# Row maxima turned by matmuls with an identity in place of DMAs, and a group's keys and queries loaded in three DMAs

## What is computed

```
layer 0:  q = x @ W_q                     4 x 512 x 320
          k, v = text @ W_k, W_v          text: the first 1020 tokens
          p = softmax(q k^T / 4)          per head, 512 x 1020
          text_out = p @ v
          qsem = p @ text                 per head, 512 x 512, then its norm
          4 image tokens: scores q k_ip^T / 4 + 0.5 * cosine(qsem, ip), softmax, times a mask, @ v_ip
          x1 = (text_out + ip_out) @ W_out + b_out + x
layer 1:  the same queries from x1; text is the first 77 tokens, the other 947 are the image part
          x2 = (softmax(text) @ v + softmax(image) @ v_ip) @ Wo^T + bo + x1
```

## Time and profile before

| | |
|---|---|
| time, median of 3 runs | 3732.37 us (3727.62 to 3734.92) |
| the profiled execution | 3733.56 us, its span 3731.7 us |
| TensorE (PE) busy | 3488.6 us, 93% |
| VectorE (DVE) busy | 2116.4 us, 57% |
| ScalarE (ACT) busy | 1689.2 us, 45% |
| GpSimd (POOL) busy | 1059.8 us, 28% |
| mean granted TensorE clock | 0.97 of full speed |
| moved by DMA | 260.59 MB in 636,270 packets |

### The profile page before, as it was taken

One profiled execution on the slowest core, in us unless ns is written; L12 is line 12 of the kernel. 1 busy time (PEld: TensorE's weight loads), 2 busy tenths in 40 slices (PEclk: granted clock), 3 DMA queues, 4 the chain that ended last, 5 costly groups with the idle time before them and its releaser, 6 DMA issues.

```text
span 3731.7 us, 66563 instructions
## 1 busy us (share of the span) xinstructions
PE 3488.6 (93%) x24208; PEld 2894.0 (78%) x24208; DVE 2116.4 (57%) x5503; ACT 1689.2 (45%) x3724; POOL 1059.8 (28%) x889
## 2 busy tenths in 40 slices
PE   5999999998999999999999999999999999999757
PEld 3888878887787877878777787787888888888535
DVE  4444445556555665655656556555655656565657
ACT  0333323444444444535444454444444555555546
POOL 1211011233332322323323222232323222322334
PEclk8999999999999999999999999999999999999878
DMA  4327423236442224226542222423642222222222
GB/s 145 112 61 55 95 67 100 64 61 76 66 112 60 59 61 115 53 52 77 65 115 53 52 62 62 114 50 60 80 55 69 55 47 49 60 52 45 51 62 46
DMA packets 636270, 260.59 MB, mean 70 GB/s; under 512 B 491852, under 2 KB 591004, under 8 KB 635938
## 3 DMA queue, kind: packets, MB, share of 16 engines
q1 hardware_dynamic: 635944, 256.33, 33.3%
HBM read 199.96 MB, written 55.44 MB: 68 GB/s over the span
## 4 chain that ended last, share of the span: by engine, by line
PE 83%; DVE 9%; issue 2%; SPq 2%; DMA 2%; ACT 1%; POOL 1%; POOLq 0%; DVEq 0%; ACTq 0%
PE acc L885 8%; PE acc L892 8%; PE acc L887 8%; PE acc L888 7%; PE acc L893 7%; PE acc L886 6%; PE score L855 4%; PE score L936 3%; PE spare L936 3%; PE av L923 3%; PE score L857 3%; PE av L927 3%; PE score L972 3%; PE spare L1008 2%; PE spare L972 2%
## 5 line engine op out<-in xcount | busy, mean ns | idle before, releaser
L1077 ACT ACTIVATE prob<-score 128x512 f32<-128x512 f32 x1219 | 729.6, 599 | 1747.1 <-PE score L857 1746.3
L1377 POOL TENSOR_TENSOR prob_lo<-prob,prob_hi 128x512 fp32r<-128x512 f32 x593 | 776.1, 1310 | 1577.7 <-ACT prob_hi L1080 1577.2
L885 PE MATMUL acc<-tok_v,prob_hi 128*128 128x300 f32 x2240 | 936.1, 418 | 6.0 <-DMA tok_v<-v_scr 5.6
L892 PE MATMUL acc<-tok_v,prob_lo 128*128 128x278 f32 (+1 forms) x2560 | 750.1, 293 | 6.2 <-DVE prob_lo L1140 6.2
L887 PE MATMUL acc<-tok_lo,prob_hi 128*128 128x256 f32 (+1 forms) x2560 | 744.4, 291 | 0.4 <-POOL tok_lo L1406 0.4
L1080 ACT ACTIVATE prob_hi<-score 128x512 fp32r<-128x512 f32 x1219 | 726.4, 596 | 0.0
L888 PE MATMUL acc<-tok_lo,prob_hi 128*128 128x256 f32 (+1 forms) x2560 | 721.9, 282 | 0.0
L893 PE MATMUL acc<-tok_v,prob_lo 128*128 128x256 f32 (+1 forms) x2560 | 720.2, 281 | 0.0
L886 PE MATMUL acc<-tok_v,prob_hi 128*128 128x256 f32 x2240 | 631.4, 282 | 0.0
L1140 DVE TENSOR_TENSOR prob_lo<-prob,prob_hi 128x512 fp32r<-128x512 f32 x687 | 502.4, 731 | 85.7 <-ACT prob_hi L1080 85.6
L885 PEld LDWEIGHTS acc<-tok_v,prob_hi 128*128 128x128 f32 x2240 | 433.0, 193 | 85.7 <-issue 58.7
(11 more groups left out here) (265 smaller groups left out, 5011.0 us busy)
## 6 DMA issues: line engine op xcount, KB each, us to landing
k_ring<-k_scr SPq DMA_DIRECT2D x960, 64.0 KB
tok_v<-v_scr SPq DMA_DIRECT2D x160, 176.0 KB, 3.3
v_ring<-v_scr SPq DMA_DIRECT2D x160, 148.5 KB, 3.3
ctx_t<-in_ctxT SPq DMA_DIRECT2D x8, 2048.0 KB, 9.3
q_ring<-q_scr SPq DMA_DIRECT2D x960, 16.0 KB
v_scr<-v_stage SPq DMA_DIRECT2D x32, 440.0 KB, 2.5
k_scr<-part_bf SPq DMA_DIRECT2D x32, 384.0 KB, 2.6
v_scr<-v_stage SPq DMA_DIRECT2D x36, 330.0 KB, 9.8
```

Of the source, the lines that this page charges most:

```text
L885: e.matmul(out_a[:, 0:SEG + VCOLS], p_hi, tok_v[0:kk, c, seg, v_lo:v_lo + SEG + VCOLS], start=first, stop=False)
L892: e.matmul(out_a[:, v_one:v_one + SEG + VH], p_lo, tok_v[0:kk, c, seg, v_lo + v_one:v_lo + v_one + SEG + VH], start=False, stop=False)
L1077: e.activation(prob[:, es, :], bank_s[:, :], ACT.Exp, scale=SCALE)
L1377: e.tensor_tensor(prob_lo[:, ps, :], prob[:, es, :], prob_hi.bitcast(F32)[:, ps, :], ALU.subtract).then_inc(s_low[1], 1)
```

## The change

The rows of maxima: `neg_max` is now split into its three parts while the queries still lie on the 128 partitions. The parts go to columns 96 to 98 (or 101) of `row_parts`, 102 columns of which the rest are zero, for each of the 4 rows. Step max_rows becomes four matmuls with a bf16 identity, whose result has each part on its own partition, 96 to 101, and 512 columns wide; one copy by VectorE brings it into `q_ring`. `max_t`, `max_bf` and the DMAs go.

Loads and stores: `q_scr` and `k_scr` hold all six products for each dimension, in the order (dimension, product), so a group's keys are one load of 96 rows, its queries another, and its constant rows a third. A store of parts becomes three DMAs: with `Q_RUNS` part 0 is written three times, part 1 twice and part 2 once; with `K_RUNS` parts 0 to 2, then 0 and 1, then 0.

The spans of the maxima change as well. At the start a bf16 identity and the zeros of `row_parts` are made.

```diff
-MAX_SPAN = {"lead": (8, 6), "woven": (11, 11), "tail": (8, 16)}
+MAX_SPAN = {"lead": (8, 4), "woven": (12, 7), "tail": (8, 9)}
...
+Q_RUNS = ((0, 3, 0), (3, 5, 1), (5, 6, 2))
+K_RUNS = ((0, 3), (3, 5), (5, 6))
...
-        q_scr = scratch("q_scr", (2 * B, 3, D, SQ), BF16)
-        k_scr = scratch("k_scr", (2 * BATCHES, 3, D, T), BF16)
+        q_scr = scratch("q_scr", (2 * B, D, 6, SQ), BF16)
+        k_scr = scratch("k_scr", (2 * BATCHES, D, 6, T), BF16)
...
@@ TensorE, first chunk of a group @@
                         e.wait_ge(s_qk[slot], qk_ready[g])
-                        e.wait_ge(s_rows[slot], rows_ready[g])
+                        e.wait_ge(s_free, job["max_rows", g] + 1)
...
@@ TensorE, step max_rows @@
-                    n_rows = MR * (layer + 1)
+                    n_rows = 96 + 3 * (layer + 1)
                     e.wait_ge(s_neg, nth["neg", g] + 1)
                     bg = bank_free(*s)
-                    e.transpose(bg[0:n_rows, 0:P], neg_max[:, layer, 0:layer + 1, :].rearrange("p a b -> p (a b)"),
-                                ident[:]).then_inc(s_bg, 1)
+                    for r in range(MR):
+                        mm = e.matmul(bg[0:n_rows, r * P:(r + 1) * P], row_parts[:, layer, r, 0:n_rows], ident_bf[:], start=True, stop=True)
+                    mm.then_inc(s_bg, 1)
...
@@ VectorE, constants @@
+                    e.tensor_copy(ident_bf[:], ident[:]).then_inc(s_mem, 1)
+                    e.memset(row_parts[:], 0.0).then_inc(s_mem, 1)
...
@@ VectorE, step split @@
-                        e.wait_ge(s_part[i % 2], 16 * (i // 2))
+                        e.wait_ge(s_part[i % 2], 48 * (i // 2))
...
@@ VectorE, step neg, behind the reduce @@
+                    value, rest = neg_max[:, layer, 0:layer + 1, :], max_r[:, layer, 0:layer + 1, :]
+                    part = row_parts[:, layer, :, 96:96 + 3 * (layer + 1)].rearrange("p r (k i) -> p i k r", i=3)
+                    e.wait_ge(s_mx, i0 + 1)
+                    e.tensor_copy(part[:, 0], value).then_inc(s_mx, 1)
+                    e.wait_ge(s_mx, i0 + 2)
+                    e.tensor_tensor(rest, value, part[:, 0], ALU.subtract).then_inc(s_mx, 1)
+                    e.wait_ge(s_mx, i0 + 3)
+                    e.tensor_copy(part[:, 1], rest).then_inc(s_mx, 1)
+                    e.wait_ge(s_mx, i0 + 4)
+                    e.tensor_tensor(part[:, 2], rest, part[:, 1], ALU.subtract).then_inc(s_neg, 1)
...
@@ VectorE, step max_rows @@
-                    e.tensor_copy(max_t[0:n, :], bank[bank_of[s]][0:n, 0:P]).then_inc(s_free, 1)
-                    e.tensor_copy(bf[:, 0, :], max_t[0:n, :]).then_inc(s_mx, 1)
-                    e.tensor_tensor(max_r[0:n, :], max_t[0:n, :], bf[:, 0, :], ALU.subtract).then_inc(s_mx, 1)
-                    e.tensor_copy(bf[:, 1, :], max_r[0:n, :]).then_inc(s_mx, 1)
-                    e.tensor_tensor(bf[:, 2, :], max_r[0:n, :], bf[:, 1, :], ALU.subtract).then_inc(s_mx, 1)
+                    e.tensor_copy(q_ring[rows, slot, :, :].rearrange("p j t -> p (j t)"), bank[bank_of[s]][rows, :]).then_inc(s_free, 1)
...
@@ SP, step lower @@
-                    e.dma_start(dst, part_bf[0:w, i % 2, :, 0:n]).then_inc(s_part[i % 2], 16)
+                        for lo, hi, j in Q_RUNS:
+                            e.dma_start(q_scr[u, rows, lo:hi, :],
+                                        part_bf[0:w, i % 2, j:j + 1, 0:SQ].broadcast_to([w, hi - lo, SQ])).then_inc(s_part[i % 2], 16)
+                        for lo, hi in K_RUNS:
+                            e.dma_start(k_scr[u // PARTS, rows, lo:hi, 512 * key[3]:512 * key[3] + 512],
+                                        part_bf[0:w, i % 2, 0:hi - lo, :]).then_inc(s_part[i % 2], 16)
...
@@ SP, step load_qk @@
-                    for j in range(GROUP):
-                        e.dma_start(k_ring[96:102, slot, j, :], row_scr[:, layer, :]).then_inc(s_qk[slot], 16)
-                    for i in range(6):
-                        rows = slice(DH * i, DH * i + DH)
-                        e.dma_start(k_ring[rows, slot, :, :],
-                                    k_scr[u // PARTS, K_PARTS[i], h0 * DH:(h0 + GROUP) * DH, :].rearrange("(h d) t -> d h t", d=DH)).then_inc(s_qk[slot], 16)
-                        e.dma_start(q_ring[rows, slot, :, :],
-                                    q_scr[u, Q_PARTS[i], h0 * DH:(h0 + GROUP) * DH, :].rearrange("(h d) t -> d h t", d=DH)).then_inc(s_qk[slot], 16)
+                    at = slice(h0 * DH, (h0 + GROUP) * DH)
+                    e.dma_start(k_ring[96:102, slot, :, :],
+                                row_scr[:, layer, :].rearrange("p (o t) -> p o t", o=1).broadcast_to([6, GROUP, T])).then_inc(s_qk[slot], 16)
+                    e.dma_start(k_ring[0:96, slot, :, :],
+                                k_scr[u // PARTS, at, :, :].rearrange("(h d) i t -> (d i) h t", d=DH)).then_inc(s_qk[slot], 16)
+                    e.dma_start(q_ring[0:96, slot, :, :],
+                                q_scr[u, at, :, :].rearrange("(h d) i t -> (d i) h t", d=DH)).then_inc(s_qk[slot], 16)
...
@@ SP, step max_rows @@
-                    for k in range(layer + 1):
-                        for i in range(3):
-                            row = 96 + 3 * k + i
-                            e.dma_start(q_ring[row:row + 1, slot, :, :].rearrange("p j (s c) -> p (j s) c", c=P),
-                                        max_bf[MR * k:MR * k + MR, layer, i, :]).then_inc(s_rows[slot], 16)
```

More of the change, by code:

```diff
@@ L24 @@
 WINDOW = 4
[L25 to L26 removed]
+PRODUCTS = 6
+Q_RUNS = ((0, 3, 0), (3, 5, 1), (5, 6, 2))
+K_RUNS = ((0, 3), (3, 5), (5, 6))
 VH = 22
@@ L608, in cross_attention_pair @@
     group_nth = [sum(1 for x in range(g) if x % RING == g % RING) + 1 for g in range(len(seq))]
-    row_loads_of = [3 if UNITS[u][0] == 0 else 6 for u, _ in seq]
-    rows_ready = [16 * sum(row_loads_of[x] for x in range(g % RING, g + 1, RING)) for g in range(len(seq))]
-    qk_ready = [16 * 14 * x for x in group_nth]
+    qk_ready = [16 * 3 * x for x in group_nth]
     score_name = ["score0" if n < tail + 3 or (n - tail) % 2 else "acc1" for n in range(len(chunks))]
@@ L675, in cross_attention_pair @@
         MR = GROUP * ST
-        max_t = sb("max_t", [2 * MR, P])
-        max_r = sb("max_r", [2 * MR, P])
-        max_bf = sb("max_bf", [2 * MR, 2, 3, P], BF16)
+        max_r = sb("max_r", [P, 2, 2, MR])
+        row_parts = sb("row_parts", [P, 2, MR, 102], BF16)
+        ident_bf = sb("ident_bf", [P, P], BF16)
         ip_scores = sb("ip_scores", [P, 2, ST, HEADS, IP])
@@ L1247, in _ @@
                     if layer == 0:
-                        e.tensor_reduce(neg_max[:, layer, 0, :], mp[:, :, 0:2], AX_X, ALU.max, negate=True).then_inc(s_neg, 1)
+                        e.tensor_reduce(neg_max[:, layer, 0, :], mp[:, :, 0:2], AX_X, ALU.max, negate=True).then_inc(s_mx, 1)
                     else:
                         e.tensor_scalar(neg_max[:, layer, 0, :], mp[:, :, 0], -1.0, None, ALU.mult)
-                        e.tensor_reduce(neg_max[:, layer, 1, :], mp[:, :, 1:3], AX_X, ALU.max, negate=True).then_inc(s_neg, 1)
+                        e.tensor_reduce(neg_max[:, layer, 1, :], mp[:, :, 1:3], AX_X, ALU.max, negate=True).then_inc(s_mx, 1)
@@ L1252, in _ @@
+                    e.wait_ge(s_mx, i0 + 3)
+                    e.tensor_copy(part[:, 1], rest).then_inc(s_mx, 1)
+                    e.wait_ge(s_mx, i0 + 4)
+                    e.tensor_tensor(part[:, 2], rest, part[:, 1], ALU.subtract).then_inc(s_neg, 1)
                 elif kind == "max_rows":
                     g = s[1]
-                    layer = UNITS[seq[g][0]][0]
-                    n, i = MR * (layer + 1), nth[s]
-                    bf = max_bf[0:n, layer, :, :]
+                    layer, slot = UNITS[seq[g][0]][0], ring_of(g)
@@ L1257, in _ @@
+                    rows = slice(96, 96 + 3 * (layer + 1))
                     e.wait_ge(s_bg, job[s] + 1)
-                    if g in same_before:
-                        e.wait_ge(s_rows[ring_of(same_before[g])], rows_ready[same_before[g]])
-                    e.tensor_copy(max_t[0:n, :], bank[bank_of[s]][0:n, 0:P]).then_inc(s_free, 1)
-                    e.wait_ge(s_free, job[s] + 1)
-                    e.tensor_copy(bf[:, 0, :], max_t[0:n, :]).then_inc(s_mx, 1)
-                    e.wait_ge(s_mx, 4 * i + 1)
@@ L1505, in _ @@
                                         v_scr[u // PARTS, :, :, c0:c0 + V1].rearrange("b p v -> p b v")).then_inc(s_v[turn % V_SLOTS], 16)
-                elif kind == "max_rows":
-                    g = s[1]
-                    layer, slot = UNITS[seq[g][0]][0], ring_of(g)
-                    e.wait_ge(s_mx, 4 * nth[s] + 4)
-                    for k in range(layer + 1):
-                        for i in range(3):
-                            row = 96 + 3 * k + i
-                            e.dma_start(q_ring[row:row + 1, slot, :, :].rearrange("p j (s c) -> p (j s) c", c=P),
```

(5 more changed lines are left out.)

19 lines of the change are left out of this document (8 added, 11 removed).

## The result

The changed kernel takes 3768.39 us (median of 4 runs, 3765.54 to 3771.69) against 3733.39 us of the kernel before (4 runs): the ratio is 1.0097 [1.0079, 1.0114]. It is 35 us slower, where 26 us less were forecast, and above the range. The profiled execution has a span of 3763.9 us.

The account below looks back on a forecast made before the run. TensorE was taken as the bound, busy 3255 of 3377 us in the long stage. Loads -19, start -6, matmuls +25, tail -22 and spans -4 gave -26 us against 3733.6, so 3706 us; range 3680 to 3731.

Parts of the forecast that it names:

- The spans: New due times of the maxima: last unit's lead stops growing, sharing VectorE's lateness over more slots; -4 us (-8 to +8).
- The cover: Slot between "neg" and max_rows hides maxima reaching TensorE 0.75 us later; where missing, mostly in the tail, waits grow 0.75 us.
- The loads: Three DMA issues a group instead of 14, 1.3 us instead of 6.4: long stage -19 us, start -6 us.
- the change doesn't save issue time: Rival on SP's queue: one issue of 96 partitions costs as much as the six it replaces; 3742 us, chance 0.04.
- The tail: Last two units of layer 1: waits for loads and row DMAs shrink; -22 us (-34 to -12).
- The four matmuls: max_rows on TensorE: 0.28 us for four, +0.17 a group over the transpose; +25 us over 145 groups.
- the load sets the pace: Rival on max_rows: weight loads of 99 and 102 columns limit the matmuls, +33 us for +25; 3714 us, chance 0.15.
- nothing overlaps: Rival on max_rows: load and matmul run one after the other, +0.47 us a group, +68 us; 3749 us, chance 0.10.
- the copy: VectorE's copy of 512 columns from PSUM into q_ring: 690 ns where the old copy took 277, +0.4 us.
- the four steps: VectorE's small split steps, now ahead of TensorE on 128 partitions: 0.2 us each where they had about 0.3.

Follow-up runs that it names:

- run 1: The changed kernel with the old spans (8, 6), (11, 11), (8, 16): 3711.26 us, 0.9919 of the kernel before.
- run 10: The changed kernel with old lead and tail spans and the woven span at (12, 11), only its length new: 3708.63 us, 0.9906 of the kernel before.
- run 9: The changed kernel with old lead and tail spans and the woven span at (11, 7), only its margin new: 3812.07 us, 1.0189 of the kernel before.
- run 3: The changed kernel, new spans kept, with max_rows two slots behind "neg" in place of one: 3723.76 us, 0.9957 of the kernel before.
- run 7: The changed kernel with the old spans and max_rows two slots behind "neg": 3682.99 us, 0.9832 of the kernel before.
- run 4: The kernel before with only the three loads a group and three stores a split; rows and spans as before: 3695.85 us, 0.9881.

## Why the prediction was wrong

**The step that failed** is "The spans": "-4 (-8 to +8, since in the long stage other pairs of jobs will meet in the two banks, and the waits for VectorE there come and go)". They cost +61.3 us: +52.7 in the woven stage, +9.5 in the tail, -1.2 in the lead and +0.3 in the start (after against run 1). I had reasoned about the tail, for which the new numbers are gentler, and gave the woven stage, three quarters of the kernel, half a bracket. With it falls the sentence ahead of it: "The cover is the slot between 'neg' and 'max_rows'; where it is missing, the wait grows by 0.75 us. That is mostly in the tail." The mechanism was named and its place was wrong. The cover was also taken for a constant, when the spans in the same diff set it: the order of the steps is fixed by `plan()`, so the work of TensorE between each "neg" and its max_rows can be added up from the list before anything runs. At about 0.72 us for a step "mix", 0.47 for "av1" and so on, a layer 1 group of the woven stage has a median of 3.1 us there with the old spans, 1.8 us with the new ones (14 groups under 0.6 us), 1.4 us with the margin of 7 and length 11, and 3.1 again with length 12 and margin 11. These are estimates, and they go with the times: runs 1 and 10 are fast, after is slow, run 9 slowest. The traces bear them out. From the start of "neg" on VectorE to the end of TensorE's work ahead of max_rows the 129 groups of the woven stage have a mean of 3.75 us in run 1, 3.61 in run 10, 2.06 in after and 1.54 in run 9; from the same start to the end of L1265 VectorE needs a mean of 1.5 to 1.7 us in all four. Under 1.5 us are 14 groups in run 1, 20 in run 10, 50 in after and 74 in run 9. The groups of L945 by form, in the woven stage of after (102 columns is layer 1, 99 is layer 0):

```profile
L945 PE MATMUL score<-ident_bf,row_parts 128*99 128x128 bf16 x168 | 17.3, 227 | 20.5 <-DVE row_parts L1265 14.1 <-DVE max_parts L1238 5.9
L945 PE MATMUL score<-ident_bf,row_parts 128*102 128x128 bf16 x148 | 15.3, 227 | 20.7 <-DVE row_parts L1265 20.7
L945 PE MATMUL spare<-ident_bf,row_parts 128*102 128x128 bf16 x112 | 11.6, 226 | 24.1 <-DVE row_parts L1265 24.1
L945 PE MATMUL spare<-ident_bf,row_parts 128*99 128x128 bf16 x88 | 9.8, 238 | 19.9 <-DVE row_parts L1265 13.6 <-DVE max_parts L1238 5.9
```

and of run 1:

```profile
L945 PE MATMUL spare<-ident_bf,row_parts 128*102 128x128 bf16 x172 | 17.3, 224 | 4.7 <-DVE row_parts L1265 4.6
L945 PE MATMUL spare<-ident_bf,row_parts 128*99 128x128 bf16 x148 | 15.4, 226 | 7.3 <-DVE row_parts L1265 7.2
L945 PE MATMUL score<-ident_bf,row_parts 128*99 128x128 bf16 x104 | 10.8, 226 | 4.7 <-DVE row_parts L1265 4.5
L945 PE MATMUL score<-ident_bf,row_parts 128*102 128x128 bf16 x92 | 9.1, 222 | 3.3 <-DVE row_parts L1265 3.3
```

Layer 1 waits 44.8 us for L1265 where run 1 has 7.9, as its shorter slot says. Layer 0 waits 27.7 us where run 1 has 11.7, though by the same count its median slot grows, from 0.95 to 1.8 us. The trace shows why the count misleads there: VectorE starts "neg" a mean of 2.05 us before TensorE comes to max_rows, where run 1 has 2.70, and it isn't held up longer from there on (1.55 us to the end of L1265, where run 1 has 1.72). It comes later to "neg"; what in its order makes it late no run shows.

The count tells what stands in the slot, too. With the old spans 30 of the 65 groups of layer 1 have four steps "mix", one "max" and one "av1" between "neg" and max_rows. With the new ones 14 have a single "av1" there, and 14 more two "mix" and the "av1".

What the new spans cost beyond these waits is open in part. With two slots they still lose 42 us (the spans of run 3 and run 7), and the waits for L1265 are then nearly equal (34.4 and 32.3 us). Of that, 33.2 us are in the woven stage, 11.6 as TensorE's busy time and 21.6 as idle. Over the span L853 waits 31.1 us in place of 7.1, and 15.4 against 1.7 of that is the wait for the copy L1271 (run 3). L934 waits about as long for VectorE to take the maxima, only for other ones of them: 33.2 us (24.0 for L1238 and 9.2 for L1240), where run 7 has 31.3 (6.4 and 24.9). The busy time and the rest of the idle time no run takes apart. It also means that the 60 us of waits for L1265 and the 61 us of loss agree only with one slot between "neg" and max_rows.

**The loads: right.** Three issues take from 34.98 to 36.13 us, 1.15 us where I said 1.3, in SP's queue of after at the start:

```profile
34.98 0.30 SPq L1485 DMA_DIRECT2D k_ring<-row_scr  x1
35.31 0.34 SPq L1487 DMA_DIRECT2D k_ring<-k_scr  x1
35.69 0.44 SPq L1489 DMA_DIRECT2D q_ring<-q_scr  x1
```

In run 4 the start is 7.8 us shorter (forecast 6), the woven stage 16.3 (forecast 19). The rival that the change doesn't save issue time is out: 96 partitions cost what 16 did. The stores write 23.6 MB more (79.04 in place of 55.44 MB; 199.96 MB are read in both), and no run shows a cost of that. One reading was off by little: the earlier trace rows counts the 1.7 us to the landing of a store from its start, and I counted them from its end. The store of x1 that I had landing at 1889.6 us landed at 1889.4.

**The tail: right with all old spans.** Run 1 is 21.9 us shorter there than before, against 22 forecast; the loads give 15.5 of it and the rows 6.4. L923's wait of 10.5 us for v_ring (L921 in the changed kernel) is down to 2.6, and L855's for the row DMAs is gone. The change as made keeps 12.4.

**The four matmuls: right, at the low end.** 0.26 us for four, +0.147 a set, where the sum had +0.17 and its bounds +0.13 and +0.23. Both rivals about them are out, the one in which the load sets the pace and the one in which nothing overlaps. The weight loads of 102 columns do take longer than those of 128, as they should by the Trainium skill ("TensorE: Matmul & The Clock Gate", "Weight-path perf modes — Fast Weight Load (FWL) and DoubleRow"), which grants the fast load only to 128 weights of a type other than fp32:

```profile
L945 PEld LDWEIGHTS score<-ident_bf,row_parts 128*102 128x102 bf16 x172 | 14.1, 129 | 45.0 <-DVE row_parts L1265 44.2
```

129 ns against 100 ns. By that rule, the trace agrees; that the load would then set the pace, the runs don't bear out.

**VectorE: the copy right, the four steps only when undisturbed.** The copy of 512 columns takes 697 ns (forecast 690). I gave the four steps 0.2 us each, and 571 of the 640 take 0.16 to 0.23 us. The other 69 take 0.46 to 2.38 us, and all of them have one thing in common: they start while GpSimd works and end within 0.05 us of the end of a GpSimd instruction, like the first cast here.

```profile
691.87 1.27 POOL L1380 TENSOR_TENSOR prob_lo<-prob,prob_hi 128x512 fp32r<-128x512 f32 x1 [1.10 <-ACT prob_hi L1079]
...
692.01 1.16 DVE L1259 CAST row_parts<-neg_max 128x8 bf16<-128x8 f32 x1
```

So from the end of the reduce to the end of L1265 it is 0.88 us (median) in the 101 groups without such a step and 1.87 us in the 59 that have one, 1.29 on average, where my sum had 0.75 for all. Of the 76 waits for L1265, 44 (59.4 of the 120.0 us) stand behind such a lengthened chain. This doesn't explain the loss, since run 1 has even more of these chains (80 of 160): they are there in both, and the spans decide whether they are covered. In all, the terms other than those of `MAX_SPAN` came to -28 us (run 1) against my -22 for them.

**The rival that was missing.** I had one on the slower side, on the price of a matmul. The mechanism that decided, a slot that the new order makes too short for a chain that the diff lengthens, stood in the text as a side remark with no price for the woven stage. 129 groups at 0.75 us would have been up to 97 us. That bound alone would have put a slower case of real weight beside the forecast.

## What to carry to other kernels

When work moves from behind a matmul to ahead of it, and the same change moves due times, compute for each instance what the waiting engine has left to do in between: in a kernel with a written order this can be read from the list of steps, and a bound of "instances x added latency" belongs in the sum until it has been. Measure the schedule constants apart from the mechanism: here the loads gave 1.2%, the new path of the maxima cost 0.35% until it had a second slot, and one margin hid both. A trace tells more of a chain than its mean: look at the spread of each step, and at what other engine ends when the long ones do. The best version has the new loads, the new rows, the old spans and max_rows two slots behind "neg" (0.9832).

## What the runs showed of the hardware

A small step of VectorE can be drawn out until an instruction of GpSimd ends: 69 of the 640 split steps of after were, and these are all that took over 0.23 us. The cast L1259 to bf16 of 4 values a partition has a mean of 502 ns in after, but a median of 179, as much as a later cast of the same size (L1263, mean 177). The mean is made by the drawn out instances. None of the 551 split steps that no GpSimd instruction overlaps takes over 0.21 us.

A TensorE wait of the same length can be followed by either clock. After the 1.83 us of idle time ahead of 1305.98 us the granted clock stayed at 1.00. After 1.83 us ahead of 1100.40 us, likewise for L1265, it was 0.58 of full speed for the next 3.9 us, near the lower of its two levels, and matmuls came 0.21 us apart in place of 0.12:

```profile
1100.40:1104.30 3.90, 3.90 (x20) 3.35 (x21) 1.81 (x3) 1.08 (x2) 1.16 (x1) 0.58 0.03 9
1104.30:1110.00 5.70, 5.70 (x46) 5.20 (x45) 3.11 (x7) 3.48 (x9) 1.28 (x1) 0.99 0.75 224
```

(Windows of after, columns as above.) So a wait can cost more than its own length, which would fit run 9: with 129.7 us of these waits in its woven stage it is also busy 27.3 us longer there than run 1 with the same instructions, at a clock of 0.98 in place of 0.99:

```profile
663.40:3567.00 2903.60, 2734.43 (x19577) 2313.97 (x19576) 1674.78 (x4254) 1354.73 (x2984) 861.26 (x708) 0.98 0.35 69
```
